# Idle matrix products between stages, two-sample transposes, and two weight products moved

## The reference

```python
# layer 0: spectral mixing, then an MLP
y = layernorm(x); X = rfft2(y)                       # 16 x 9 frequencies
X = relu(block_diagonal(X, w1) + b1)                 # 8 blocks of 12 channels, complex
h = irfft2(X); x0 = x + h + mlp(layernorm(h))        # 96 -> 384 -> 96, gelu
# layer 1: gated Toeplitz convolution along both axes
n = srms(x0); u = silu(n @ Wu + bu); v = silu(n @ Wv + bv)
x1 = x0 + (u * (toeplitz_h(v) + toeplitz_w(v))) @ Wo + bo
# layers 2 and 3: four GRU directions over the 256 places, each of 96 units
n = layernorm(x); xin, z = split(n @ w_in.T)
for each of 4 GRUs: r, k, c = gates(xin @ wih.T, h @ whh.T); h = (1 - k) * c + k * h
x = x + combine(hidden states, silu(z)) @ w_out.T
```

## Time and profile before

| | |
|---|---|
| runs | 969.74, 969.42, 963.02 us; median 969.42 |
| the profiled execution | 969.3 us, of which the span of its instructions is 967.1 |
| mean granted TensorE clock | 0.584 of full speed |
| busy | PE 917.3, PEld 817.8, DVE 813.4, ACT 711.7, POOL 27.1 us |
| transfers | 13.15 MB, mean 14 GB/s |

### The profile page before, as it was taken

The page is one execution under the profiler, slowest core; times in us unless marked ns, Lnnn a source line. Parts: engine busy times, 40 slices in busy tenths (PEclk is TensorE's granted clock), DMA queues, the critical chain, the costliest instruction groups (busy, mean ns, idle before and its releaser), DMA issues. The chain is left out here.

```text
span 967.1 us, 54906 instructions
## 1 busy us (share of the span) xinstructions
PE 917.3 (95%) x22310; PEld 817.8 (85%) x22310; DVE 813.4 (84%) x5089; ACT 711.7 (74%) x4754; POOL 27.1 (3%) x18
## 2 busy tenths in 40 slices
PE   6879798999999999999999889999999999999996
PEld 5646786699999999999999758999999999999996
DVE  7663258688888889999999977888888899999996
ACT  5453671777777777888888748777777788888884
POOL 2000250000000000000000000000000000000000
PEclk9788799755555555555555576555555555555556
DMA  5000620000000000000000000000000000000001
GB/s 155 3 16 1 122 62 10 2 4 5 4 4 5 4 5 4 4 5 4 5 5 4 4 7 3 5 4 4 5 4 4 5 4 4 4 5 4 5 4 35
DMA packets 15006, 13.15 MB, mean 14 GB/s; under 512 B 12374, under 2 KB 13911, under 8 KB 14463
## 3 DMA queue, kind: packets, MB, share of 16 engines
q1 hardware_dynamic: 14753, 9.65, 4.2%
HBM read 8.81 MB, written 0.83 MB: 10 GB/s over the span
## 5 line engine op out<-in xcount | busy, mean ns | idle before, releaser
L1338 PE MATMUL L3s_cand_sum<-states,L_w_hidden 97*128 97x8 bf16 x2048 | 174.3, 174 | 0.0
L1338 PE MATMUL L2s_cand_sum<-states,L_w_hidden 97*128 97x8 bf16 x2048 | 173.1, 174 | 0.0
L1338 PE MATMUL L2s_reset_sum<-states,L_w_hidden 97*128 97x8 bf16 x2048 | 142.2, 180 | 2.6 <-DVE states L1182 1.7
L1338 PE MATMUL L3s_reset_sum<-states,L_w_hidden 97*128 97x8 bf16 x2048 | 142.1, 180 | 2.5 <-DVE states L1182 1.7
L1338 PEld LDWEIGHTS L3s_cand_sum<-states,L_w_hidden 97*128 97x128 f16 x2048 | 132.6, 104 | 0.0
L1338 PEld LDWEIGHTS L2s_cand_sum<-states,L_w_hidden 97*128 97x128 f16 x2048 | 131.9, 104 | 0.0
L1338 PE MATMUL L3s_keep_sum<-states,L_w_hidden 97*128 97x8 bf16 x2048 | 130.0, 174 | 0.0
L1338 PE MATMUL L2s_keep_sum<-states,L_w_hidden 97*128 97x8 bf16 x2048 | 130.0, 174 | 0.0
L1279 ACT ACTIVATE L2s_reset<-L2s_reset_sum 96x16 f32<-96x16 f32 x512 | 92.8, 181 | 45.9 <-PE L2s_reset_sum L1338 45.8
L1279 ACT ACTIVATE L3s_reset<-L3s_reset_sum 96x16 f32<-96x16 f32 x512 | 92.9, 181 | 45.2 <-PE L3s_reset_sum L1338 45.0
L1338 PEld LDWEIGHTS L2s_reset_sum<-states,L_w_hidden 97*128 97x128 f16 x2048 | 101.9, 110 | 28.0 <-DVE states L1182 4.9
(11 more groups left out here) (257 smaller groups left out, 3071.6 us busy)
## 6 DMA issues: line engine op xcount, KB each, us to landing
L_wih_raw<-in_L_wih SPq DMA_DIRECT2D x2, 1152.0 KB, 11.4
lagged<-in_L_w SPq DMA_DIRECT2D x1, 1296.0 KB, 8.2
L_w_hidden_raw<-in_L_whh SPq DMA_DIRECT2D x2, 576.0 KB
stream<-in_x SPq DMA_DIRECT2D x2, 384.0 KB, 3.8
out<-stream SPq DMA_DIRECT2D x4, 192.0 KB, 2.1
l_idft<-in_idft SPq DMA_DIRECT2D x1, 400.0 KB
rpe_lw<-in_rpe_lw SPq DMA_DIRECT2D x1, 384.0 KB
lagged<-coefs SPq DMA_DIRECT2D x16, 24.0 KB, 2.0
```

Of the source, the lines that this page charges most:

```text
L1338: return e.matmul(dst, weights.hidden[0:rows, wp, GATES * (2 * g + j) + gate, :], rhs, start=False, stop=False, skip_group_check=True)
```

## The change

Three things are changed, and what they need around them.

1. Idle products: `idle_products` issues fp32 products of the identity with itself, 128x128x128, into a bank that nobody reads; they wait for nothing. The ten at the kernel's start were there before. New are four at the end of `mix_frequencies`; in `mlp` six at the start, one behind each fourth transpose, two behind the last, and six at the end; in `toeplitz` eight at the start, one behind each fourth transpose, three behind the last, and five at the end: 42 in all.
2. The mixed spectrum is stored with a pitch of 64 instead of 36, in a buffer shared with `rows`, `spatial` and `residual`, so that one transpose takes two samples: 32 transposes with 128 stationary columns instead of 64 with 36. Of each bank, VectorE copies one sample of each pair and ScalarE the other, 16 copies each as before. The inverse products wait for all copies of both. `rpe.normalise(0)` stands after the second of the five evictions instead of after the last, and `rpe.turn(0)` and its copy after all transposes and copies.
3. `W` 0 and `W` 1 of `L3`, with their high parts, `rest` products and low parts, are made at the end of `toeplitz`, where the two pairs of throwaway products were. In `L2` the order is `W` 0, `W` 1, eight transposes, `rest` 0 and 1, `W` 2, eight transposes, `rest` 2; in `L3` it is `W` 2, 16 transposes, `rest` 2. `minus` is made once.

```diff
+def idle_products(e, bank, ident, count):
+    for _ in range(count):
+        e.matmul(bank[:, 0:P], ident[:], ident[:], start=True, stop=True)
...
+        if i % 4 == 3:
+            idle_products(e, idle_bank, ident, 1)
...
+        mixed_wide = shared[:, 0:BLOCKS * BATCH * 64].rearrange("p (a f) -> p a f", f=64)
+        mixed = mixed_wide[:, :, 0:FQ]
...
+        def turned_part(n, s, pair):
+            src = banks[n % TURN_BANKS][64 * s:64 * s + FQ, :].rearrange("p (b j m) -> p b j m", b=4, j=QUARTERS)
+            dst = by_freq[64 * pair:64 * pair + FQ, s::2, n, :].rearrange("p b (j m) -> p b j m", j=2)
+            return dst, src[:, :, 2 * pair:2 * pair + 2, 0:COMPLEX]
...
-                rpe.normalise(e, 0)
-                for m in range(0, 16, 2):
+                    if k == 1:
+                        rpe.normalise(e, 0)
+                for n in range(BLOCKS):
...
-                for m in range(16):
-                    n, b0 = m // 2, 4 * (m % 2)
+                for n in range(BLOCKS):
                     e.wait_ge(relu_done, n + 1)
...
-                        last = e.transpose(banks[m % TURN_BANKS][0:FQ, b * P:(b + 1) * P], mixed[:, n * BATCH + b0 + b, :], ident[:])
+                        last = e.transpose(banks[n % TURN_BANKS][:, b * P:(b + 1) * P],
+                                           flat(mixed_wide[:, n * BATCH + 2 * b:n * BATCH + 2 * b + 2]), ident[:])
                     last.then_inc(turned, 1)
-                    if m == 9:
-                        rpe.turn(e, 0)
+                rpe.turn(e, 0)
                 e.wait_ge(turn_saved_v, 16)
+                e.wait_ge(turn_saved_s, 16)
...
+                idle_products(e, banks[5], ident, 4)
...
-                transposes(e, norm, ident, banks, turned)
+                idle_products(e, banks[6], ident, 6)
+                transposes(e, norm, ident, banks, turned, banks[6])
+                idle_products(e, banks[6], ident, 2)
...
+                idle_products(e, banks[0], ident, 6)
...
+                idle_products(e, banks[7], ident, 8)
+                transposes(e, norm, ident, banks, turned, banks[7])
+                idle_products(e, banks[7], ident, 3)
...
+                e.activation(minus[:], ident[0:C, 0:C], ACT.Copy, scale=-1.0).then_inc(first_saved, 1)
+                for b in range(2):
+                    later.high(e, b, bank(LATER + b))
+                for b in range(2):
+                    later.low(e, b, bank(LATER + b))
...
                     if k % 2 == 0:
-
-                        e.wait_ge(gated, 3 * half + 1)
-                        for _ in range(2):
-                            e.matmul(bank(OUT + k)[0:C, :], w_u[:, 0:C], xT[0:C, 0:BANK], start=True, stop=True)
+                        e.wait_ge(both_added, 3 + half)
+                        later.product(e, half, bank(LATER + half))
+                    if k == 2:
+                        e.wait_ge(first_saved, CHUNKS * NB + 1)
+                        later.rest(e, 0, bank(LATER), minus)
                     e.wait_ge(gated, 4 * (half + 1))
...
+                later.rest(e, 1, bank(LATER + 1), minus)
+                idle_products(e, banks[2], ident, 5)
...
+    def product(self, e, b, bank):
+        for m in range(CHUNKS):
+            last = e.matmul(bank[0:C, :], self.inner[:, m, :], self.raw[:, m, b * BANK:(b + 1) * BANK],
+                            start=(m == 0), stop=False, skip_group_check=True)
+        last.then_inc(self.summed, 1)
...
+                if done == 0:
+                    for b in range(2):
+                        weights.product(e, b, banks[4 + b])
+                else:
+                    weights.product(e, 2, banks[6])
                 turn(range(0, 8))
-                weight_product(1)
+                if done == 0:
+                    for b in range(2):
+                        weights.rest(e, b, banks[4 + b], minus)
+                    weights.product(e, 2, banks[6])
                 turn(range(8, 16))
-                weight_product(2)
...
+                weights.rest(e, 2, banks[6], minus)
```

More of the change, by code:

```diff
@@ L364, in _ @@
                 e.wait_ge(ident_loaded, 16)
-                for _ in range(WARM):
-                    e.matmul(banks[0][:, 0:P], ident[:], ident[:], start=True, stop=True)
+                idle_products(e, banks[0], ident, 10)
                 e.wait_ge(loaded, 48)
@@ L865, in _ @@
                 back(1)
+                e.wait_ge(later.raw_loaded, 32)
                 for k in range(NB):
@@ L896, in __init__, with part, high, rest @@
         self.raw_loaded = ctx.enter_context(nc.semaphore(f"{layer}_raw_loaded"))
+        self.summed = ctx.enter_context(nc.semaphore(f"{layer}_w_summed"))
+        self.parted = ctx.enter_context(nc.semaphore(f"{layer}_w_parted"))
+    HIGH, LOW = (1, 2, 5), (3, 4, 6)
+    def part(self, part, b):
+        return self.input[0:C, part].rearrange("p n q -> p (n q)")[:, b * BANK:(b + 1) * BANK]
+    def product(self, e, b, bank):
[3 more added lines that the diff above has]
+        last.then_inc(self.summed, 1)
+    def high(self, e, b, bank):
+        e.wait_ge(self.summed, self.HIGH[b])
+        e.activation(self.part(0, b), bank[0:C, :], ACT.Copy).then_inc(self.parted, 1)
+    def rest(self, e, b, bank, minus):
+        e.wait_ge(self.parted, self.HIGH[b])
+        e.matmul(bank[0:C, :], minus[:], self.part(0, b), start=False, stop=True, skip_group_check=True).then_inc(self.summed, 1)
+    def low(self, e, b, bank):
+        e.wait_ge(self.summed, self.LOW[b])
+        e.activation(self.part(1, b), bank[0:C, :], ACT.Copy).then_inc(self.parted, 1)
 class WeightSplit:
@@ L931, in lo, with gru_layer @@
         e.wait_ge(self.lo_ready, 2)
-def gru_layer(nc, d, layer, stream, ident, lagged, weights, stats, forward, states, bias_rows, out_dram=None, stored=None):
+def gru_layer(nc, d, layer, stream, ident, minus, lagged, weights, done, stats, forward, states, bias_rows, out_dram=None, stored=None):
     with ExitStack() as outer:
@@ L972, in gru_input @@
         GATE_BANKS = (7, 0, 4, 5, 6)
-        part_of = lambda part, b: weights.input[0:C, part].rearrange("p n q -> p (n q)")[:, b * BANK:(b + 1) * BANK]
+        w_parted = weights.parted
         with nc.Block() as block:
@@ L1025, in input_high @@
                                  scale=affine[:, 0:1], bias=affine[:, 1:2]).then_inc(hi_ready, 1)
[L1027 removed]
+                if done == 0:
+                    for b in range(2):
+                        weights.high(e, b, banks[4 + b])
+                else:
+                    weights.high(e, 2, banks[6])
                 input_high(0)
                 input_high(1)
[L1030 removed]
+                if done == 0:
+                    for b in range(2):
+                        weights.low(e, b, banks[4 + b])
+                    weights.high(e, 2, banks[6])
                 input_high(2)
                 input_high(3)
[L1033 to L1035 removed]
+                weights.low(e, 2, banks[6])
                 e.wait_ge(w_loaded, 16)
@@ L1044, in _ @@
             def _(e):
-                def weight_product(b):
-                    for m in range(CHUNKS):
-                        last = e.matmul(banks[4 + b][0:C, :], weights.inner[:, m, :], weights.raw[:, m, b * BANK:(b + 1) * BANK],
-                                        start=(m == 0), stop=False, skip_group_check=True)
-                    last.then_inc(w_summed, 1)
                 def turn(tiles):
```

98 lines of the change are left out of this document (37 added, 61 removed).

## The result

After the change the kernel takes 956.75 us in the median of 11 executions (954.75 to 962.67), against 966.36 us (963.02 to 970.34, 11 executions) before: a ratio of 0.9912, 95% interval [0.9885, 0.9939]. The prediction was 956 in a range of 951 to 963. The time lies where it was put, but the gain is 9.6 us and not 13.4, since the 969.3 us from which the sum was made is 3 us above the median of before over more executions. By the ratio it stays just within the 1% to which the text gave 0.25. That the time came out within 1 us of 956 is luck in part: the base was 3 us too high and the gain nearly 4 us too small.

A forecast was written before the change was run, and what follows sets the result against it. Both recurrences (739 of 967.1 us, half clock) stay; the other 228 us hang on TensorE's clock after borders. Terms -3.3 - 2.7 - 3.4 + 0.2 - 3.2 - 1.2 = -13.6 from 969.3 gave 956, range 951 to 963.

The forecast's parts named there:

- the 1% to which the text gave 0.25: Whole kernel: change of time within 9.7 us, about what a measurement can tell from no change; chance 0.25.
- The mixed spectrum: Before the MLP: 32 transposes in place of 64 let the inverse products start at 45.5, not 48.75; -3.3 us.
- The memset that is added lies on GpSimd, idle from 8 us on: Mixed spectrum: the added memset was put on an idle engine and given no cost in the sum.
- Had the clock come back at once at 41.4: Mixed spectrum: case where before would be bound by VectorE, its copies done at 47.3, and the gain 1.9 us.
- MLP: Border to the MLP: clock falls about 67.7, is back near 71; 12 records take 5.2 us; -2.7 us.
- Transposes don't count: Rival: clock returns only in the dense products behind the transposes, MLP starts 1.0 late and as slow; 967 us; 7%.
- Third stage: Border to the third stage: w_v products start at 106.5 at full clock, -4.3, or at 108.0, -2.8; taken as -3.4 us.
- Third layer's input: L2's input: full clock through the border and new W order; ScalarE ends at 181.0, not 184.24; -3.2 us.
- The end of the third stage: Output products: W products replace throwaway ones at the same cost, and a new rest product adds time; +0.2 us.
- Last layer: L3's input: clock half at 566.2, back only at 579.8, ScalarE's last at 583.1; -1.2 us; if back at 573, -3.5.
- The rival that the borders go cold: Clock still falls at the borders and the change gives half of its gain there; 961 us; 20%.
- faster by over 1%: Whole kernel: faster by more than 9.7 us, below 959.7 us; chance 0.73.

The follow-up runs named there:

- third group: Kernel after again (955.49 us, 0.9905), and it with two mends (memset on ScalarE, gap filled; 0.9918), recurrence gaps also filled (0.9874), and second xT copy added (0.9897).
- the halves: Kernel before with the 42 idle products alone (963.05 us, 0.9976); kernel after without its 42 new idle products (962.24 us, 0.9970).
- the second execution: Another profiled execution of the unchanged kernel after: 952.83 us, span 950.8; that kernel's median beside it 955.49 us, 0.9905.

## Why the prediction was right or wrong

**The recurrences and the mechanism: right.** The recurrences took 369.4 us each in both executions (368.7 each in all four profiled executions of the third group, whatever the kernel), and what was gained lies around them, where the clock held across the borders. No single part brings it: 0.24% and 0.30% for the halves, 0.74% together.

**The mixed spectrum: the wait right, its price wrong.** The step "start at 45.5 and not at 48.75: -3.3" came to +0.3. "The memset that is added lies on GpSimd, idle from 8 us on" cost it at nothing, and it cost 0.7 of the 0.3 - (-3.3) = 3.6 that were missing: it held line 123, as moving it showed. Then 0.8 us went on the way up to the first transpose (39.44 against 37.95, less the 0.7); they belong to no edit, since in the second execution it stands at 37.78. The wait for the copies went nearly as put, 8.0 us behind the first transpose where 10.8 had been and 7.6 was forecast (ScalarE's 16 copies took 5.6 us from first to last, 5.2 of them busy, and not 5.1). But I had not asked what the idle time ahead of the inverse products, 0.41 us before and 1.53 after, does to the clock: it fell, and eight records took 4.54 in place of 2.93 us, 1.6 more. These four make 0.7 + 0.8 + 0.5 + 1.6 = 3.6. In the second execution the term was -3.0.

But both figures, and the forecast's -3.3, are set against one execution of before, in which the clock came back only at 43.9. The forecast had named the other case, "Had the clock come back at once at 41.4", with the inverse products at 47.3. The kernel with idle products alone has the mixed spectrum of before, and in its profiled execution the clock was back at 41.7; TensorE's timeline:

```profile
47.34 2.93 PE L421 MATMUL l_bank<-l_by_freq,l_idft 100*128 100x384 f32 x8 [0.40 <-DVE l_by_freq L316]
```

That is 9.6 us behind its first transpose (37.77), where the new order needs 8.0 in every profiled execution: 1.5 saved and not 2.8, of which the memset takes 0.7 back. The inverse products end at 59.5 there, and between 57.9 and 61.9 in the eight executions that have the new transposes and the memset on GpSimd. So where the clock is back early, this part gives nearer to 1 us than to 3. In how many executions that is so isn't shown.

**MLP: right, at its better end.** -3.6 against -2.7, with the bound "the clock never falls, -3.8". This and the gain of the third stage are the idle products' alone: with nothing but them the two stages take 33.6 and 21.0 us, as in the kernel after, and with the transposes alone 37.2 and 23.1, as before. In the second execution of the kernel after, the clock fell from 65.1 to 68.6, about where the forecast had it fall (67.7), and the stage took 34.2, -3.0. The rival *Transposes don't count* said 1.0 late and as slow: the 12 records took 5.42 us, so this rival fell. The Trainium skill, "TensorE: Matmul & The Clock Gate", "Part 4: PE-mode transpose", would have the clock stay low through transposes; it rose at 44.75, after transposes alone from 39.44. The wider transposes cost no more: in the second execution the last 15 of them start from 41.36 to 42.89, one in 0.109 us at full clock, where the earlier trace rows give 0.117 for the narrow ones. The prediction read from this that the trace disagrees with a load that grows with the columns; what it shows is only that the pace does not: the loads themselves are listed at 98 ns with 36 columns (before, 45.6 to 48) and at 141 with 128 (second execution, 41.5 to 43).

**Third stage: a term mis-sized.** -2.0 against -3.4. The clock held, the products started in time, and the products "at 0.65 for each of 16 groups" were 12.53 us and not 10.3: the 0.65 came from ScalarE's pace in the last groups, which read neighbouring columns, and I applied it to the strided ones as well. In the trace before, half of the strided ones ran at half clock, where the stride does not show: 15 in 4.80 us from 107.3, 0.32 each. But the clock was back at 112.2, so the other half stood there at full clock, in a row that I had not asked for. TensorE's loads before, from 112.3 to 115.5:

```profile
L815 PEld LDWEIGHTS l_bank<-l_w_v,l_xT 97*128 97x128 f32 x15 | 3.4, 314 | 0.0
```

From 116 on, over neighbouring columns, they are listed at 190. With neighbouring columns throughout, the products took 10.64 us and the stage 19.1: -3.9. (The prediction's 121.1 less 116.9 is 4.2, and not 4.3.)

**Third layer's input: right.** -3.4 against -3.2. It has two parts: with idle products alone, at full clock and in the old order, it takes 17.6 us, so the clock gives 1.6 and the new order 1.8 more. The end of the third stage came as forecast, +0.2.

**Last layer: the clock was full.** -3.4 against -1.2, near the bound "-3.5". The forecast took the clock at the first `W` product from the one execution of before, where it was half at 566.2. There it had risen in `L2`'s output products, at 562.7, and fallen again at 566.1. In the kernel after it rose in the same products, at 553.3, and held over the border. No part of the change lies in `L2`'s recurrence or output, so where the clock rises there is not its doing. But I had taken the rarer case: the eight profiled executions with this last layer and no idle products around `L2`'s output give 15.0 to 15.1 five times, and 16.4, 16.8 and 17.8 once each. The forecast's own case does occur. The kernel with the moved memset, whose last layer is that of the kernel after, shows in its windows and its TensorE timeline:

```profile
556.10:569.50 13.40, 12.12 (x34) 5.65 (x33) 11.04 (x31) 8.86 (x16) 0.00 (x0) 0.50 0.03 7
...
563.25 8.50 PE L1120 MATMUL L3i_bank<-forward,L3i_gate_parts 96*96 96x512 f16 x24 [0.93 <-DVE forward L1053]
```

There the gate products take 8.50 us, and the input 17.8, -0.6. That *moving* the products brought the gain of 3.4 is not so: unmoved, in the new order, it was 15.45 in both executions. With idle products alone, in the old order and with the clock at half over the border, it was 18.3, so no run tells here what the order gives and what the clock.

**The sum's base.** "The profiled execution agrees with the median (969.42)" rested on three runs. With more, the median before is 966.36, and 964 to 965 beside the experiments. This is why 0.73 stood on faster by over 1%. The rival that the borders go cold gave 961; four of 11 executions after lie at 961.0 to 962.7. Their mean granted clocks are 0.588, 0.589, 0.591 and 0.594, those of the other seven 0.593 to 0.604. So three of the four had less of the full clock than any other, which fits the rival; at which border they lost it is open, since the profiled one was another.

**Open.** In how many executions the clock falls at which border; why idle products alone gain 1.9 us in the median though the clock is held in all twelve executions; whether transposes and idle products help each other; what of the last layer's gain is the order's and what the clock's.

## What to carry to other kernels

Products at half clock hide other costs, here the stride of a stationary operand, and these come out when the clock is raised: price each operation by a row at the clock, and with the operand, that it will have. A gain read against one execution can be that execution's own bad luck with the clock, as in the mixed spectrum: look for the same stage in a second one. Filling a wait with idle products is free only where the queue behind them is not needed, and it does not rule out a fall of the clock; judge it by medians of many executions, as one profile can be several us off. An added instruction on an idle engine is not free by that alone: look at what the busy engines do in the same stretch.

## What was not expected of the hardware

- A `tensor_scalar` of VectorE on 128x16 fp32 took 0.94 us beside a memset of GpSimd, and 0.17 alone.
- fp32 stationary operands with a stride of 16 columns load in 309 ns and not 190 at full clock.
- The clock fell over a wait of 1.53 us (from 48.2) in one execution and held over one of 2.42 us in another of the same kernel.
- The recurrences kept TensorE busy for 366.6 of 369.4 us, at half clock but for their first 2 to 5 us. Idle products of 3.76 us behind the first were followed by output products of 4.36 us in place of 6.14, those behind the second by 6.74 in place of 5.94.
